# Cross attention ahead of a routed expert layer: the context used raw, its mean and deviation applied elsewhere

## The chip, the core and the metric

One core of a Trainium2 chip runs the whole program. The metric is device time in microseconds (us), the median of several executions. TensorE is written PE, VectorE DVE, ScalarE ACT, GpSimd POOL; SP (SyncE) issues most DMAs. All data is float32.

## The reference, cut to what matters

There are 32 batches of 100 query rows (256 wide) and 361 context rows (192 wide).

```
def layernorm(x, g, b):
    mu = jnp.mean(x, axis=-1, keepdims=True)
    var = jnp.mean(jnp.square(x - mu), axis=-1, keepdims=True)
    return (x - mu) * jax.lax.rsqrt(var + EPS) * g + b
x1 = layernorm(modality1, ln1_g, ln1_b)      # modality1 = layernorm of x
x2 = layernorm(modality2, ln2_g, ln2_b)      # modality2 = ctx_768, 32 x 361 x 192
q = x1 @ Wq + bq
k = x2 @ Wk + bk
v = x2 @ Wv + bv
scores = jnp.einsum('bqe,bke->bqk', q, k) * scaling
attn = jax.nn.softmax(scores, axis=-1)
ctx = jnp.einsum('bqk,bke->bqe', attn, v)
return ctx @ Wo + bo
```

The result is added to x. A second layer follows: a plain layernorm, one shared expert and 31 routed experts of which each row takes its best 3 (softmax over 31 logits, two 256 by 256 products with an exact gelu), summed and added.

## The kernel before, in words

The program has two stages. In the attention stage 37 numbered steps (-2 to 36, `STEPS`, line 275) are unrolled on each engine. Step i works on several things at once: the statistics of context batch i+2, the normalization of batch i+1, the scores of batch i-1, the softmax weights and the mix of batch i-2, and, for those steps in which a tile of 128 rows begins or ends (`starts`, `ends`, lines 106 and 110), the queries of a tile, the output of attention (`ends(i - 2)`), its layernorm (`ends(i - 3)`) and its routing (`ends(i - 4)`). Of the 32 batches 25 end a tile. After the stage come the 105 tiles of the routed experts and a final sum; the change leaves those alone.

Every engine works through its own instructions in order and waits on semaphores. What follows is the order within one step.

- SP (lines 341 to 371): loads context batch i+4 (288 KB, four buffers, line 322), the rows of a tile, in step 24 (`FILL_STEP`) a fill of 3.3 MB (line 349) with three small ones (lines 352, 353), in steps 1 to 23 one expert's first matrix and in steps 1 to 18 one expert's second matrix (256 KB each, lines 359, 365), and stores two tiles of 128 KB once DVE has made them (lines 370, 371).
- POOL (lines 505 to 536): the deviation of batch i+2 to the power -1/2 (lines 510, 512), the running mask sum (line 520), the same power for the output tile (lines 525, 527), and three indirect stores of 128 rows (line 535) for the tile of `ends(i - 4)`.
- DVE (lines 688 to 809): logits of a tile (701), statistics of context batch i+2 (705), layernorm of the output (724, which waits for line 527 of the step before), normalization of context batch i+1 into a buffer `z` (732, three instructions), normalization of x (743), aggregation of the statistics (763, 765), the routing mask (773), the row maximum of the scores (778), then, after the wait for the output product of PE, the output tile and the end of the routing (782 to 809).
- PE (lines 1015 to 1092): transposes of the softmax weights of batch i-2 (1026), six transposes of the normalized context of batch i (987, 988), scores (1039, 1040: 128 and 65 rows deep, the last row is a constant one that carries the key bias), the mix (1051, 1054), the query product, rank (1080, 1081, which wait for the mask of line 773), output product (1085, 1086) and logits.
- ACT (lines 573 to 635): copies PE's results to SBUF. Two copies of 361 columns carry the transposed context (595, 596).

Before step 0, DVE folds the biases into the key and value weights (`wk_aug`, `wv_aug`, lines 833 to 841) and PE multiplies query by key weights and value by output weights, so that a context row needs no product of its own.

## Time and profile before

| | us |
|---|---|
| median of 3 executions | 519.08 (519.04 to 521.75) |
| the profiled execution | 518.88 |
| its span in the trace | 517.1 |
| PE busy | 465.7 (90%) |
| DVE busy | 350.8 (68%) |
| POOL busy | 322.8 (62%) |
| ACT busy | 246.9 (48%) |

The span is what the trace shows between the first and the last instruction; the time of the same execution is 1.8 us longer. "Busy" counts instructions under way, and a busy PE isn't a PE at its peak. The shares are means over both stages. The page cuts the span into 40 slices of 12.9 us; the attention stage with its lead-in fills the first 18 or so.

### The profile page before, as it was taken

The numbers are of one execution on the slowest core, as the hardware profiler recorded it, in microseconds if no ns is written. First come the engines' busy times: TensorE is split into PE (matmuls) and PEld (weight loads), VectorE is DVE, ScalarE is ACT, GpSimd is POOL, SyncE is SP. The second block draws the span as 40 slices with busy tenths as digits, with TensorE's granted clock in tenths as the row PEclk, the third lists the DMA queues.
The fourth block names the chain that finished last, engine by engine and source line by source line (L and its number), as shares of the span: only waits on it lengthen the run. The fifth ranks groups of instructions, "written<-read, shape, count | busy, mean of one in ns | idle before, by whom it ended". The sixth has DMA issues, their size and how long they took to land.

```text
span 517.1 us, 13549 instructions
## 1 busy us (share of the span) xinstructions
PE 465.7 (90%) x3204; PEld 409.2 (79%) x3204; DVE 350.8 (68%) x1556; ACT 246.9 (48%) x821; POOL 322.8 (62%) x363
## 2 busy tenths in 40 slices
PE   1898889898888898888899999999999999999891
PEld 1787678687676777767798999989999999999891
DVE  4748788777868688657466766666666666661684
ACT  1355555646464565646344545545454545553220
POOL 6213756747567575657168888778888888885000
PEclk9989999989898999999999999999999999999997
DMA  7464766767565982569369999979888888875998
GB/s 240 125 194 125 250 207 194 237 187 231 191 200 181 324 291 94 168 208 320 97 122 189 187 186 189 185 132 145 136 138 138 135 138 137 138 116 83 332 349 305
DMA packets 80621, 97.53 MB, mean 189 GB/s; under 512 B 8689, under 2 KB 65298, under 8 KB 80546
## 3 DMA queue, kind: packets, MB, share of 16 engines
q1 hardware_dynamic: 60786, 70.79, 45.5%
q0 software_dynamic: 19472, 25.61, 29.3%
q8 instruction: 29, 0.48, 0.4%
q14 instruction: 46, 0.38, 0.3%
q10 hardware_dynamic: 288, 0.27, 0.2%
HBM read 54.91 MB, written 41.73 MB: 187 GB/s over the span
## 4 chain that ended last, share of the span: by engine, by line
PE 44%; DVE 7%; DMA 5%; SPq 4%; issue 3%; POOL 1%; ACT 1%; POOLq 0%; DVEq 0%
PE bank L1184 16%; PE bank L1195 15%; PE bank L1173 4%; DMA sum<-y_sb,token 3%; DMA w_all<-sum 2%; SPq L449 2%; SPq L450 1%; SPq L448 1%; POOL sum L557 1%; DVE w_all L732 1%; PE bank L1101 1%; DMA xt<-expert_rows_in 1%; PE bank L1085 1%; PE bank L1110 1%; PE bank L1051 1%
## 5 line engine op out<-in xcount | busy, mean ns | idle before, releaser
L557 POOL DMA_INDIRECT sum<-y_sb,token x105 | 169.8, 1617 | 48.6 <-issue 22.6
L643 ACT ACTIVATE up<-bank,b_all 128x128 f32<-128x128 f32 x260 | 81.4, 363 | 103.5 <-PE bank L1184 66.5
L1184 PE MATMUL bank<-xtt,w1b 128*128 128x128 f32 x840 | 111.2, 275 | 1.1 <-DVE w1b L913 0.8
L1195 PE MATMUL bank<-w_all,up 128*128 x420 | 108.6, 381 | 0.0
L1184 PEld LDWEIGHTS bank<-xtt,w1b 128*128 128x128 f32 x840 | 102.1, 192 | 1.7 <-ACT xtt L669 1.6
L921 DVE TENSOR_SCALAR y_sb<-bank,gate,inverse 128x256 f32<-128x256 f32 x105 | 57.1, 543 | 54.3 <-PE bank L1195 53.8
L535 POOL DMA_INDIRECT expert_rows_in<-xt,slot x75 | 74.6, 995 | 25.3 <-issue 25.0
L1195 PEld LDWEIGHTS bank<-w_all,up 128*128 128x128 f32 x420 | 71.7, 191 | 5.6
L913 DVE COPY w1b<-w_all 128x512 f32 x105 | 46.9, 447 | 18.2 <-PE bank L1184 8.0
L669 ACT ACTIVATE xtt<-bank 128x256 f32<-128x256 f32 x105 | 40.1, 383 | 38.3 <-PE bank L1173 37.7
L1173 PE MATMUL bank<-ident,xt 128*128 128x128 f32 x210 | 40.1, 273 | 0.2 <-DMA xt<-expert_rows_in 0.2
L1173 PEld LDWEIGHTS bank<-ident,xt 128*128 128x128 f32 x210 | 29.3, 141 | 11.4 <-DMA xt<-expert_rows_in 1.2
L512 POOL TENSOR_TENSOR rs<-rs,mhalf 128x4 f32<-128x4 f32 x32 | 33.2, 1036 | 2.5
L1051 PEld LDWEIGHTS bank<-w_all 128*128 128x128 f32 (+1 forms) x192 | 26.5, 192 | 9.3 <-ACT w_all L581 1.0
L600 ACT ACTIVATE tok<-bank 128x100 f32<-128x100 f32 x32 | 8.1, 253 | 53.5 <-PE bank L1054 53.5
L732 DVE TENSOR_SCALAR w_all<-w_all,mv,rs 128x192 f32<-128x192 f32 x96 | 32.3, 392 | 0.2 <-POOL rs L512 0.2
L608 ACT ACTIVATE w_all<-bank,negmax 100x361 f32<-100x361 f32 x32 | 17.9, 561 | 25.6 <-DVE negmax L778 25.6
L705 DVE BATCH_NORM_STATS2 c<-w_all 128x6 f32<-128x192 f32 x96 | 27.8, 345 | 3.4 <-POOL gates_all L494 3.4
L510 POOL TENSOR_TENSOR rs<-mv,eps_cols 128x4 f32<-128x4 f32 x32 | 6.7, 208 | 36.8 <-DVE mv L765 36.4
L1039 PE MATMUL bank<-w_all,tok 128*100 128x361 f32 x64 | 27.3, 512 | 0.0
L1110 PE MATMUL bank<-w_all,up 128*128 128x256 f32 x100 | 26.0, 382 | 1.5 <-DVE w_all L968 1.4
L1091 PEld LDWEIGHTS bank<-wr_s,tok 128*128 128x128 f32 x100 | 13.8, 193 | 17.0 <-ACT tok L616 16.6
(180 smaller groups left out, 938.3 us busy)
## 6 DMA issues: line engine op xcount, KB each, us to landing
xt<-expert_rows_in SPq DMA_DIRECT2D x105, 132.0 KB, 2.9
w_all<-in_w SPq DMA_DIRECT2D x47, 256.0 KB, 4.9
w_all<-in_ctx SPq DMA_DIRECT2D x32, 288.0 KB, 3.0
w_all<-sum SPq DMA_DIRECT2D x15, 384.0 KB, 7.4
sum<-pad_rows SPq DMA_DIRECT2D x1, 3328.0 KB, 12.0
w_all<-in_x SPq DMA_DIRECT2D x25, 128.0 KB, 3.3
sum<-y_sb SPq DMA_DIRECT2D x25, 128.0 KB, 3.7
sum<-xt SPq DMA_DIRECT2D x25, 128.0 KB, 3.8
```

The source lines that it names most:

```text
L512: pool.tensor_tensor(rs[s][:, 1, :], rs[s][:, 0, :], mhalf[:, :], ALU.pow).then_inc(ctx_rstd, 1)
L535: pool.indirect_dma_start(xs, bass.IndirectOffsetOnAxis(ap=slot[s4][:, k:k + 1], axis=0), h_sb[s4][:, :], None).then_inc(scattered[s4], 16)
L557: pool.indirect_dma_start(sums[s], bass.IndirectOffsetOnAxis(ap=token[sx][:, 0:1], axis=0), y_sb[sx][:, :], None, compute_op=ALU.add).then ...
L643: ins = act.activation(up[s][:, m * P:m * P + P], up_ps[s][:, m * P:m * P + P], ACT.Gelu, bias=b1_all[:, e, m:m + 1].rearrange("p o n -> p ...
L669: act.activation(xtt[s][:, :], tile_ps[s], ACT.Copy).then_inc(tile_t_copied, 1)
L732: ins = dve.tensor_scalar(z[s4][:, k, 0:D2], c_sb[s4][:, k, :], mv[s][:, k, 0:1], rs[s][:, 1, k:k + 1], ALU.subtract, ALU.mult)
L913: dve.tensor_copy(w1b[n.slot(2)][:, :], w1_all[:, bass.ds(e, 1), :].rearrange("p o n -> p (o n)"))\
L921: dve.tensor_scalar(y_sb[sx][:, :], down_ps[s], gate[s][:, 0:1], inverse[s][:, 0:1], ALU.mult, ALU.mult).then_inc(y_made, 1)
L1051: pe.matmul(mix_ps[:, 0:LQ], z[s4][0:KT[k], k, 0:P], probs_t[s][0:KT[k], k, :], start=(k == 0), stop=(k == 2))
L1173: mm = pe.transpose(tile_ps[s][:, c * P:c * P + P], xt[sx][:, c * P:c * P + P], ident[:, :])
L1184: mm = pe.matmul(up_ps[s][:, m * P:m * P + P], w[:, c * INTER + m * P:c * INTER + m * P + P], xtt[s][:, c * P:c * P + P], start=(c == 0), ...
L1195: mm = pe.matmul(down_ps[s], up[s][:, m * P:m * P + P], w, start=(m == 0), stop=(m == 1))
```

## The change

The context is no longer normalized row by row and no longer transposed on the core. The following comes in its place.

- The host also gives the context transposed (`ctxt`). SP loads it straight into the tiles that the scores read as keys (`load_ct`, 96 rows by two times 361), in three buffers, and the raw rows into six buffers (`load_ctx`, now batch i+3 in step i, once the mix of batch i-3 is made).
- The mean is taken out of the weights: `weights_with_bias` multiplies the key and the value weights by the layernorm's gain and subtracts each row's mean, so that a raw context row gives the same product as a centred one. It has four reductions over 192 columns and three small or medium instructions where there were two reductions. It runs for the keys before step -1 and for the values after step 0.
- POOL makes, beside the power -1/2, the deviation itself, twice (two more `tensor_tensor`): once as a row for the scores, once as column 192 of the raw context, where the constant one was.
- SP stores both rows (key deviation to the power -1/2, and deviation) to DRAM in runs of three numbers (`store_key_rows`), and loads them back in the next step: the first one to 100 partitions (`rb`), the second as the last row of the transposed keys (`load_key_rows`).
- DVE multiplies the scores by `rb` and takes the maximum in one instruction with SBUF output, then negates the maximum in a small one. ACT's exponential reads that output. ACT scales the transposed softmax weights by the power -1/2 (three instructions for two).
- Keys are dealt to the three blocks with a stride of 3 (121, 120 and 120 of them), and the width 192 is cut in 96 and 96 (+1) instead of 128 and 64 (+1).
- The 41 early expert loads are spread over 30 steps; one late load of four experts is merged into the one of step 33.

```
-        c_sb = [lend(2, P, 3 * D2).rearrange("p (t d) -> p t d", d=D2) for _ in range(SLOTS)]
-        zt0, zt1 = [lend(2, P, LK) for _ in range(2)], [lend(2, D2C, LK) for _ in range(2)]
-        z = [lend(2, P, 3 * (D2 + 1)).rearrange("p (t d) -> p t d", d=D2 + 1) for _ in range(SLOTS)]
+        ct = [lend(2, D2C, 2 * LK).rearrange("p (c j) -> p c j", c=2) for _ in range(CTS)]
+        c_sb = {s: lend(2, P, 3 * (D2 + 1)).rearrange("p (t d) -> p t d", d=D2 + 1) for s in (2, 3, 4, 5, 0, 1)}
...
             def load_ctx(b):
-                if b >= SLOTS:
-                    sp.wait_ge(ctx_norm, b + 1 - SLOTS)
+                if b >= CS:
+                    sp.wait_ge(mix_made, b + 1 - CS)
                     alone(sp)
...
+            def load_ct(b):
+                if b >= CTS:
+                    sp.wait_ge(scores_made, b + 1 - CTS)
+                    alone(sp)
+                sp.dma_start(ct[b % CTS][0:H, :, :], ctx_t[b].rearrange("(c p) j -> p c j", p=H)).then_inc(ct_in[b % CTS], 16)
+
+            def store_key_rows(b):
+                sp.wait_ge(ctx_std, 2 * b + 2)
+                alone(sp)
+                sp.dma_start(key_rows[b].rearrange("k (p t) -> p k t", t=3), rs[b % RS][:, 1:3, 0:3]).then_inc(key_rows_out, 16)
+
+            def load_key_rows(b):
+                sp.wait_ge(key_rows_out, 16 * (b + 1))
+                if b >= CTS:
+                    sp.wait_ge(max_made, b + 1 - CTS)
+                alone(sp)
+                sp.dma_start(rb[b % CTS][:, :], key_rows[b, 0, 0:LK].partition_broadcast(LQ)).then_inc(rb_in[b % CTS], 16)
+                sp.dma_start(ct[b % CTS][H:D2C, 1, :], key_rows[b, 1:2, 0:LK]).then_inc(ct_in[b % CTS], 16)
...
             def step(i):
-                if batch(i + 4) is not None:
-                    load_ctx(i + 4)
+                if batch(i + 3) is not None:
+                    load_ctx(i + 3)
                 if starts(i + 4) is not None:
                     load_x(starts(i + 4))
+                if batch(i + 1) is not None:
+                    load_ct(i + 1)
+                    load_key_rows(i + 1)
+                if batch(i + 2) is not None:
+                    store_key_rows(i + 2)
                 if i == FILL_STEP:
...
+                for w_all, w, e in EARLY[len(EARLY) * (i - 1) // EARLY_STEPS:len(EARLY) * i // EARLY_STEPS] if 1 <= i <= EARLY_STEPS else []:
+                    sp.dma_start(w_all[:, e, :], w[e]).then_inc(expert_in, 16)
...
@@ pool
+                    pool.wait_ge(ctx_rstd, b + 1)
+                    pool.tensor_tensor(rs[r][:, 2, 0:3], rs[r][:, 0, 0:3], rs[r][:, 1, 0:3], ALU.mult).then_inc(ctx_std, 1)
+                    pool.tensor_tensor(c_sb[b % CS][:, :, D2], rs[r][:, 0, 0:3], rs[r][:, 1, 0:3], ALU.mult).then_inc(ctx_std, 1)
...
@@ scalar
-                    act.activation(zt0[s], zt_ps0[:, 0:LK], ACT.Copy)
-                    act.activation(zt1[s], zt_ps1[0:D2C, 0:LK], ACT.Copy).then_inc(ctx_t_copied, 1)
...
+                    for k in range(3):
+                        ins = act.activation(probs_t[s][0:KEYS[k], k, :], probs_ps[0:KEYS[k], k * LQ:(k + 1) * LQ], ACT.Copy,
+                                             scale=rs[b % RS][0:KEYS[k], 1, k:k + 1])
...
@@ vector
-                    for k in range(3):
-                        ins = dve.tensor_scalar(z[s4][:, k, 0:D2], c_sb[s4][:, k, :], mv[s][:, k, 0:1],
-                                                rs[s][:, 1, k:k + 1], ALU.subtract, ALU.mult)
-                    ins.then_inc(ctx_norm, 1)
...
-                    dve.tensor_reduce(negmax[s][:, :], bank[s][0:LQ, 0:LK], AX.X, ALU.max, negate=True).then_inc(rowmax_made, 1)
+                    dve.wait_ge(rb_in[rated % CTS], (rated // CTS + 1) * 16)
+                    if rated >= 2:
+                        dve.wait_ge(probs_transposed, rated - 1)
+                    dve.tensor_tensor_reduce(probs[s][:, 0:LK], bank[s][0:LQ, 0:LK], rb[rated % CTS][:, :], 1.0, LOWEST, ALU.mult, ALU.max,
+                                             rowmax[s][:, 0:1]).then_inc(max_made, 1)
...
+                    dve.tensor_scalar(negmax[s][:, :], rowmax[s][:, :], -1.0, None, ALU.mult).then_inc(rowmax_made, 1)
...
+            def weights_with_bias(w_aug, bias, k):
+
+                for c in range(2):
+                    dve.tensor_tensor_reduce(bank[2 * k][:, c * D2:c * D2 + D2], w_aug[:, c, 0:D2], b2_row, 1.0, bias[:, c:c + 1], ALU.mult,
+                                             ALU.add, w_aug[:, c, D2:D2 + 1])
+                for c in range(2):
+                    ins = dve.tensor_tensor_reduce(bank[3][:, c * D2:c * D2 + D2], w_aug[:, c, 0:D2], g2_row, 1.0, 0.0, ALU.mult, ALU.add,
+                                                   wsum[k][:, c:c + 1])
+                then(ins)
+                then(dve.tensor_scalar(wmean[k][:, :], wsum[k][:, :], -1.0 / D2, None, ALU.mult))
+                for c in range(2):
+                    ins = dve.tensor_scalar(w_aug[:, c, 0:D2], bank[3][:, c * D2:c * D2 + D2], wmean[k][:, c:c + 1], None, ALU.add)
+                return ins
...
@@ tensor
-            def turn_ctx(b):
-                s4 = b % SLOTS
-                pe.wait_ge(ctx_norm, b + 1)
...
-                    pe.wait_ge(ctx_t_copied, b + 1)
+                    pe.wait_ge(ct_in[b % CTS], (b // CTS + 1) * 32)
...
-                    pe.matmul(bank[s][0:LQ, 0:LK], tok[:, 0, of_batch(b)], zt0[s], start=True, stop=False)
+                    pe.matmul(bank[s][0:LQ, 0:LK], tok[0:H, 0, of_batch(b)], ct[b % CTS][0:H, 0, :], start=True, stop=False)
```

## Rows read from the trace of the kernel before

**Rows 1.** The page's 40 slices of the span, and the first DMA queue.

```profile
PEclk9989999989898999999999999999999999999997
...
DMA  7464766767565982569369999979888888875998
...
GB/s 240 125 194 125 250 207 194 237 187 231 191 200 181 324 291 94 168 208 320 97 122 189 187 186 189 185 132 145 136 138 138 135 138 137 138 116 83 332 349 305
...
q1 hardware_dynamic: 60786, 70.79, 45.5%
```

**Rows 2.** Busy time by stretch: all scores, and five steps at the full clock.

```profile
core 0: us, PE busy (x) PEld busy (x) DVE busy (x) ACT busy (x) POOL busy (x), PEclk, DMA share, GB/s
...
20.95:223.46 202.51, 179.87 (x1264) 148.67 (x1262) 154.34 (x728) 110.55 (x411) 119.30 (x186) 0.96 0.64 203
...
186.99:218.80 31.81, 28.64 (x214) 23.60 (x212) 25.13 (x120) 18.40 (x71) 20.70 (x32) 1.00 0.46 154
```

**Rows 3.** Timeline of PE: start, duration, line; in brackets the wait.

```profile
20.95 0.77 PE L1039 MATMUL bank<-w_all,tok 128*100 128x361 f32 x2
...
131.42 0.27 PE L987 MATMUL bank<-ident,w_all 128*128 128x128 f32 x1
...
132.04 0.77 PE L1039 MATMUL bank<-w_all,tok 128*100 128x361 f32 x2
...
135.89 0.19 PE L1080 MATMUL bank<-mask,tri 128*128 128x31 bf16 x1 [1.08 <-DVE mask L773]
...
223.46 0.77 PE L1039 MATMUL bank<-w_all,tok 128*100 128x361 f32 x2
```

**Rows 4.** Timeline of DVE over two full steps.

```profile
133.37 0.95 DVE L732 TENSOR_SCALAR w_all<-w_all,mv,rs 128x192 f32<-128x192 f32 x3
...
135.40 0.28 DVE L765 BATCH_NORM_AGGREGATE mv<-c 128x2 f32<-128x6 f32 x3
...
135.59 0.24 DVE L773 TENSOR_REDUCE mask<-picks 128x31 bf16<-128x93 f32 x1
...
135.75 0.52 DVE L778 TENSOR_REDUCE negmax<-bank 100x1 f32<-100x361 f32 x1
...
137.11 0.17 DVE L782 RECIPROCAL rinv<-bank 128x1 f32<-128x1 f32 x1 [0.84 <-PE bank L1086]
...
142.33 0.25 DVE L773 TENSOR_REDUCE mask<-picks 128x31 bf16<-128x93 f32 x1
```

**Rows 5.** Timeline of POOL in the same stretch.

```profile
138.66 0.19 POOL L525 TENSOR_TENSOR rrs<-rmv,eps_cols 128x1 f32<-128x1 f32 x1 [1.41 <-DVE rmv L809]
...
139.67 1.04 POOL L535 DMA_INDIRECT expert_rows_in<-xt,slot  x1 [0.19 <-issue]
...
143.26 0.22 POOL L510 TENSOR_TENSOR rs<-mv,eps_cols 128x4 f32<-128x4 f32 x1
...
144.59 0.23 POOL L520 TENSOR_TENSOR msum<-msum,mask 128x31 bf16<-128x31 bf16 x1
```

**Rows 6.** DMA issues of the page: KB each, median us to landing.

```profile
w_all<-in_ctx SPq DMA_DIRECT2D x32, 288.0 KB, 3.0
...
sum<-pad_rows SPq DMA_DIRECT2D x1, 3328.0 KB, 12.0
```

**Rows 7.** Timeline of SP's DMA queue around the fill of step 24.

```profile
168.60 0.39 SPq L349 DMA_DIRECT2D sum<-pad_rows  x1
...
169.04 7.57 SPq L352 DMA_DIRECT2D sum<-pad_rows  x2
...
180.67 1.21 SPq L322 DMA_DIRECT2D w_all<-in_ctx  x1
```

**Rows 8.** Timeline of DVE during the folding of the weights.

```profile
9.40 0.42 DVE L834 CUSTOM_DVE_ANT_0 bank<-w_all,cols_s 128x192 f32<-128x192 f32 x1
...
9.74 0.49 DVE L837 CUSTOM_DVE_ANT_0 bank<-w_all,cols_s 128x256 f32<-128x256 f32 x1
```

More of the change, by code:

```diff
@@ L27 @@
 EPS = 1e-5
+LOWEST = -3.0e38
 SCALE = float(E) ** -0.5
-D2B = D2 - P
-D2C = D2B + 1
-KT = [P, P, LK - 2 * P]
+H = D2 // 2
+D2C = H + 1
+KEYS = [len(range(k, LK, 3)) for k in range(3)]
 TOKENS = B * LQ
@@ L194, in program @@
+        g1_s, bq_s, bk_s, bv_s = (cols_s[:, 2 * k:2 * k + 2] for k in range(4))
         uq = sb("uq", [P, 2])
         fold_q = sb("fold_q", [P, 2, D2 + 1])
-        fold_o0, fold_o1 = sb("fold_o0", [P, D1 + 1]), sb("fold_o1", [D2C, D1 + 1])
-        qs0, qs1 = sb("qs0", [P, 2]), sb("qs1", [D2C, 2])
+        fold_o0, fold_o1 = sb("fold_o0", [H, D1 + 1]), sb("fold_o1", [D2C, D1 + 1])
+        qs0, qs1 = sb("qs0", [H, 1]), sb("qs1", [D2C, 1])
+        wsum, wmean = two("wsum", [P, 2]), two("wmean", [P, 2])
@@ L239, in program @@
         x_in = sems(*[f"x_in{s}" for s in range(8)])
-        c_in = sems(*[f"c_in{s}" for s in range(SLOTS)])
+        c_in = sems(*[f"c_in{s}" for s in range(CS)])
+        ct_in = sems(*[f"ct_in{s}" for s in range(CTS)])
+        rb_in = sems(*[f"rb_in{s}" for s in range(CTS)])
         h_out = sems(*[f"h_out{s}" for s in range(SLOTS)])
@@ L271, in program @@
         sum_made, final_made, final_out = sems("sum_made", "final_made", "final_out")
-        MADE = 23
+        MADE = 19
         LATE = 21
         STEPS = range(-2, B + 5)
-        w1_order, w2_order = list(range(EARLY1)), list(range(EARLY2))
+        EARLY = [(w2_all, w2, e) for e in range(10)]
+        EARLY += [p for e in range(8) for p in ((w1_all, w1, e), (w2_all, w2, 10 + e))] + [(w1_all, w1, e) for e in range(8, EARLY1)]
+        EARLY_STEPS = 30
+        assert len(EARLY) == EARLY1 + EARLY2
         FILL_STEP = 24
-        EXPERT_DMAS = EARLY1 + EARLY2 + 8
+        EXPERT_DMAS = EARLY1 + EARLY2 + 7
         PADS_SP, PADS_POOL = range(0, 20), range(20, NE)
@@ L467, in _ @@
             const(pool.memset(eps_cols[:, 3:4], EPS * EPS / (1.0 + EPS)))
-            for s in range(SLOTS):
-                const(pool.memset(z[s][:, :, D2:D2 + 1], 1.0))
             const(pool.memset(ident[:, :], 0.0))
@@ L1029, in step @@
                     turn_x(starts(i))
-                if i > 0 and batch(i) is not None:
-                    turn_ctx(i)
                 b = batch(i - 1)
```

209 lines of the change are left out of this document (89 added, 120 removed).

## The prediction

> **What bounds the kernel now.** I read the page's 40 slices first: PE's granted clock, the share of the DMA engines and the bytes [rows 1]. The change touches only the attention stage. There the DMA engines work at 0.4 to 0.9 of their time, with one slice at 0.9 in the middle; nowhere for long at the limit. The table of stretches comes second: from the first scores to the last are 202.5 us, in which PE is busy 180, DVE 154, POOL 119, ACT 111 [rows 2]. No engine is full, so I look for a cycle. The timelines come third. Scores start at 20.95 for batch 0 and at 223.46 for batch 31 [rows 3]: 202.51 / 31 = 6.53 us per step.
>
> In a full step (all tile work present) the reader sees DVE without a gap except for one wait, at line 782, for PE's output product; and PE waits at line 1080 for DVE's mask [rows 3, 4]. From one mask to the next are 142.33 - 135.59 = 6.74 us: DVE's tail and head up to the mask, then PE's rank and output product, then DVE's tail again. That is the cycle. PE's own work isn't in it, except for the part from the mask to line 782. Once the clock was granted at 0.96 on average rather than 1.00 [rows 2]; over five undisturbed steps a step takes 31.81 / 5 = 6.36, so about 0.17 per step is the price of half-speed spells.
>
> POOL has a cycle of its own, close behind: from line 525 at 138.66 to the end of line 520 at 144.59 + 0.23 are 6.16 us of nearly gapless work, 3.6 of it for the three indirect stores (139.67 to 143.26) [rows 5]. Its statistics come from line 765, just before the mask [rows 4]. The cycle fits under 6.74 with 0.6 to spare. That slack is what the whole prediction turns on.
>
> **The change, part by part.** The sum is made against the profiled execution, 518.88 (span 517.1, 1.8 around it), 0.2 under the median.
>
> PE. Six transposes go: 132.04 - 131.42 = 0.62 us per step [rows 3], 19 us over 31. They stand where PE soon waits 1.08 for the mask, so on the path they are worth little in full steps. Narrower weight loads (97 and 97 for 128 and 65) are small: 0 to 0.15 per step, taken at 0. The strided reading of the softmax weights isn't in the trace: 0 to 0.3 per step (three transposes at the pace of the six are 0.3), taken at 0.
>
> ACT. Two copies go, three small instructions stand for two; ACT is busy 111 of 202 us [rows 2] and gets shorter. Nothing.
>
> DVE. Three normalizations go: 0.95 busy, about 0.9 in place [rows 4]. The row maximum, 0.52, becomes a reduction with a product. The nearest rows are line 834 with 0.42 for 192 columns and line 837 with 0.49 for 256 [rows 8]; by their slope 361 columns take about 0.60. It stands between mask and line 782, beside PE's rank and product (135.75 + 0.52 to 137.11, 0.84 of waiting [rows 4]), so it costs nothing until it grows by 0.8. The small negation, about 0.15, is in the cycle. The full cycle becomes 6.74 - 0.9 + 0.15 = 6.0. If only this counted, steps would be 0.75 shorter: 31 x 0.75 = 23 us.
>
> POOL. Two more products of three columns. Line 525, 0.19, is the nearest row [rows 5]; with the wait for the power before them I take 0.45 per step (0.2 to 0.7). POOL's full cycle becomes 6.16 + 0.45 = 6.6, over DVE's 6.0. DVE's line 724 waits for line 527 of the step before, so POOL now sets full steps, 25 of 32. In the others it has no stores and catches up: its mean is (25 x 6.6 + 7 x 1.8) / 32 = 5.6. Between 5.8 (POOL hidden by its catching up) and 6.6.
>
> SP. This is a new wait with a long queue behind it. Within step i-1, SP waits for POOL's deviation of batch i+1 (`store_key_rows`), and behind that wait stand the weights, the two stores, and the next `load_ctx(i + 3)`, which DVE needs at the start of step i+1. In the timeline POOL starts its power only after the stores, at 143.26, and ends at 144.6 [rows 5]; with the added products that is about 6.5 after the step's start (137.11 + 1.45). Then SP's issues: one store, one or two weights, two tiles, the load, some five at 0.4 (line 349 takes 0.39 [rows 7]), 2.2 in all, and 3.0 to land [rows 6], 4.5 under more load. Sum 11.7 to 13.2 for two steps, less 0.2: 5.8 to 6.5 per step where stores are on POOL in both. It lies on POOL's cycle, not beside it, so a late POOL delays the load too. Three buffers ahead of the mix don't help, since the queue is in order.
>
> DMA. Added per batch are 277 KB of transposed keys, 141 KB of `rb`, and 256 pieces of 12 bytes. 13.4 MB in all against 203 GB/s x 202.5 us = 41 MB now: by bytes, 0.64 of the engines' time becomes 0.64 x 54 / 41 = 0.85 [rows 2]. By packets, the first queue's take 0.455 x 16 x 517.1 / 60786 = 62 ns each [rows 1]; 292 long ones and 256 short ones of at most that are 1.1 to 2.1 us of 16 engines per step, 0.81 to 0.97. The early weights, spread out, take a little off. Hidden on average; transfers land later. The page "DMA: Bandwidth & Descriptors" of the Trainium skill says in "Why a DMA increments its semaphore by 16 and not by 1" that a transfer is split over the largest number up to 16 that divides its rows, so 100 partitions use 10 engines; and under "Specifications" that pieces under 512 bytes are read, modified and written. No trace of before shows either; both would put the first ten engines nearer to full, and by them I would set the step toward 6.6.
>
> I take 6.40 per step, the middle of 5.8 and 6.6 drawn up by the two chains meeting and by the half-speed spells, 0.17. Gain: 31 x (6.53 - 6.40) = 4. Bounds: 5.8 gives 23, 6.7 gives a loss of 5.
>
> The fill. Before, SP issues it at 168.60; the small one behind it is held for most of 7.57, and the next context load goes out only at 180.67, 12.1 later [rows 7]. That load is batch 29, read in step 27 (about 193): hidden. After the change the fill stands behind step 24's wait for POOL, so about 6.5 + 0.5 = 7.0 after DVE's start of step 24, and the load behind it is batch 28, which DVE reads in step 26, 2 x 6.4 + 0.2 = 13.0 after that start. It goes out at 7.0 + 12.1 + 0.8 (a weight) = 19.9 and lands at 22.9: a stall of 10 us of DVE, with PE idle soon after. Even counted from the fill's landing, 12.0 [rows 6], it is 19.0 + 3.0 - 13.0 = 9. If POOL has no stores ahead, 1.3 less; catching up gives back 1 to 2. Between 6 and 13; taken at 10.
>
> Start. The key weights take two more reductions (0.34 apart) and three instructions, some 1.7, before PE's first fold; the value folds leave PE's path, 2 us. Between -1 and 2, taken at 0.5. The late expert loads end before the experts start either way: 0, at most 2.
>
> Sum: 518.9 - 4 + 10 + 0.5 = 525.4; 525.5.
>
> **The rivals.**
>
> 1. DVE's cycle alone decides. POOL catches up in the seven short steps, SP's chain stays under two steps, and the step is 5.8. For it: POOL's mean of 5.6, and POOL idle 83 of 202 us now [rows 2]. Against: the short steps stand singly between runs of three or four full ones, where POOL loses 0.6 each. The fill then costs about 9, since DVE runs faster toward it. 518.9 - 23 + 9 = 505. Faster.
>
> 2. The fill is hidden as before, by a queue that holds more or by a DVE that is late itself, and the step is 6.4: 518.9 - 4 + 1 = 516. Against: the order of SP's issues is fixed, and rows 7 show it held.
>
> 3. The DMA engines become the bound (slower by more). One mechanism: `rb` and the keys land after PE's step i+2 wants them. It decides once landing takes longer than about 8 us. For it: slices at 0.9 even now [rows 1], and the fill at landing 12.0. Price: steps of 6.8, 31 x 0.27 = 8, and a fill of 12: 539.
>
> 4. The saving on PE counts fully, and more (PE no longer pushed to half speed): that is case 1 with 3 us more, 502. It goes with case 1. The opposite, more waiting on PE and so more half-speed spells (each costs about a microsecond where it meets a product), is within the 0.17 above.
>
> **How the numbers follow.** Forecast 0.48 (own range 519 to 533), rival 1 with 4 0.26, rival 2 0.12, rival 3 0.14. What the measurement can tell from no change is 0.5%, 516.5 to 521.7. Faster: 0.26 + 0.06 from rival 2 + 0.01 = 0.33. Same: 0.06 + 0.07 from the forecast's low end = 0.13. Slower: 0.40 + 0.14 = 0.54. The range reaches into rivals 1 and 3: 504 to 537.
>
> **What would show it.** Right: a wait of DVE's context statistics (or PE's idle time) of 6 to 13 us at step 26, a few us after the fill, released by a DMA of the context; POOL without idle time for DVE's aggregation in full steps; DVE waiting for POOL's power at line 724's successor; scores 6.3 to 6.5 apart elsewhere; the DMA share of the stage at 0.8 or more. Wrong: steps of 5.8 with DVE waiting only for PE (rival 1); no gap after the fill (rival 2); PE or DVE waiting for `ct` or `rb` in ordinary steps (rival 3). The forecast is wrong by more than its range if SP's chain misses two steps everywhere.

## The result, and the profile after

| | before | after |
|---|---|---|
| median, us (4 executions each, side by side) | 519.06 (513.79 to 521.75) | 561.21 (559.04 to 562.90) |
| ratio, 95% interval | | 1.086 [1.0798, 1.0922] |
| the profiled execution, us | 518.88 | 560.7 |
| its span | 517.1 | 558.1 |
| mean granted clock of PE | 0.977 | 0.935 |

Slower by 42 us. Ratios here and below leave disturbed runs out, so they aren't always the quotient of the medians. The forecast of 525.5 had the direction, and its range ended at 537.

The page after, read as [rows 1] were: PE's busy share by slice, PE's granted clock, the DMA engines, the first DMA queue.

```profile
PE   0898879688686872888889989999999999999992
...
PEclk9997897979989796699899999999999999999997
DMA  7888798879997899868944999998998888886998
...
q1 hardware_dynamic: 79714, 84.48, 56.9%
```

Two things catch the eye in slices 5 to 18: the DMA engines mostly at 0.8 to 0.9, where they were mostly at 0.5 to 0.7, and a clock below 0.9 in 7 of the 14. The first was expected, and it is the tempting culprit. The second goes with idle time of PE, which the next table shows: 183 us busy of 239.

The table of stretches, with the columns of [rows 2]: all scores (22.56 is the first, 262.04 the last), the part ahead of the fill, and the one step behind the fill.

```profile
22.56:262.04 239.48, 182.82 (x1091) 142.95 (x1091) 133.91 (x705) 91.12 (x350) 129.44 (x246) 0.87 0.86 225
22.56:205.06 182.50, 145.33 (x880) 113.76 (x880) 109.47 (x578) 73.54 (x282) 103.17 (x199) 0.90 0.88 219
205.06:226.67 21.61, 8.04 (x39) 6.41 (x38) 4.36 (x21) 2.86 (x11) 6.06 (x12) 0.67 0.99 306
```

The stage went from 202.51 to 239.48, or 37.0 of the profiled 41.8. The first scores start 1.6 later; what comes behind the last scores is 558.1 - 262.04 = 296.1 against 293.6, 2.4 more; the time around the span is 0.8 more. One step, behind the fill, takes 21.61. The other 30 take (239.48 - 21.61) / 30 = 7.26 each, against 6.53 before. So the ordinary steps are the larger part: 30 x (7.26 - 6.53) = 22, and the step behind the fill 15. DVE and ACT do 20 us less work each than before in the stage, POOL 10 more, and all of them wait more: no engine is busy all the time.

The list of waits after: engine, line, released by, total us, times, longest. PEld is PE loading the weights of a product.

```profile
ACT w_all L628 <- DVE negmax L801: 76.1, 31, 16.4
...
DVE rinv L797 <- PE bank L1108: 44.3, 21, 4.2
...
DVE c L725 <- DMA w_all<-in_ctx: 37.3, 14, 13.0
PEld bank L1113 <- ACT tok L636: 36.4, 24, 1.9
```

Three of them have a counterpart before, and all three have grown:

```profile
DVE rinv L782 <- PE bank L1086: 31.5, 22, 2.7
ACT w_all L608 <- DVE negmax L778: 25.6, 24, 3.0
...
PEld bank L1091 <- ACT tok L616: 16.6, 18, 1.7
```

They are ACT's wait for the negated maximum (L628, before L608), DVE's for PE's output product (L797, before L782) and PE's for ACT's copy of the transposed output tile (L1113, before L1091). New is DVE's wait for the context (L725). One part of it is on the page: a context load now lands 6.3 us after its issue (median) where it was 3.0 [rows 6].

```profile
w_all<-in_ctx SPq DMA_DIRECT2D x32, 289.5 KB, 6.3
```

The other part is in the waits of SP, which the page doesn't list (line 86 is a helper through which SP's waits pass):

```profile
SPq L86 <- DMA key_rows<-rs: 61.8, 26, 4.6
...
SPq L86 <- POOL w_all L540: 43.2, 19, 6.4
```

SP stands 61.8 us for the landing of the key rows that it has just stored, and 43.2 for POOL's second product of the deviation. Neither wait existed before, and everything that SP loads stands behind them.

Three timelines of one full step show how ACT's, DVE's and PE's waits hang together. DVE:

```profile
138.93 0.88 DVE L725 BATCH_NORM_STATS2 c<-w_all 128x6 f32<-128x192 f32 x3 [1.32 <-DMA w_all<-in_ctx]
...
141.00 0.50 DVE L792 CUSTOM_DVE_ANT_0 w_all<-bank,rb 100x361 f32<-100x361 f32 x1
141.43 0.08 DVE L792 DVE_READ_ACCUMULATOR2_ANT rowmax<- 100x1 f32 x1
142.56 0.17 DVE L797 RECIPROCAL rinv<-bank 128x1 f32<-128x1 f32 x1 [1.05 <-PE bank L1108]
142.65 0.13 DVE L801 TENSOR_SCALAR negmax<-rowmax 100x1 f32<-100x1 f32 x1
```

ACT, which waits for that negation:

```profile
142.81 0.60 ACT L628 ACTIVATE w_all<-w_all,negmax 100x361 f32<-100x361 f32 x1 [2.80 <-DVE negmax L801]
143.32 0.36 ACT L636 ACTIVATE tok<-bank 128x256 f32<-128x256 f32 x1
```

PE, which waits for ACT's copy:

```profile
141.93 0.60 PE L1108 MATMUL bank<-fold_o,tok 97*128 97x257 f32 x2
143.73 0.63 PE L1113 MATMUL bank<-wr_s,tok 128*128 128x31 f32 x4 [1.21 <-ACT tok L636]
```

The reader sees the maximum finished at 141.51 and its negation, 0.13 us of work, at 142.65. Between them DVE stands at L797, which waits for PE's output product. The negation has nothing to do with that product; it is only behind it in the code. ACT's exponential (L628) waits for the negation, ACT's copy of the transposed output tile (L636) stands behind the exponential, PE's logits (L1113) wait for the copy, and all of PE's next step stands behind the logits. Before, the maximum negated itself ahead of DVE's wait [rows 4]; ACT's exponential then started 0.8 us before DVE's reciprocal, which started at 137.11, and now starts 0.25 after it. The row of ACT before:

```profile
136.31 0.56 ACT L608 ACTIVATE w_all<-bank,negmax 100x361 f32<-100x361 f32 x1 [1.29 <-DVE negmax L778]
```

A new cycle has closed: PE's output product, DVE's negation, ACT's exponential and copy, PE's logits, PE's next step.

SP's queue and DVE around the fill, as in [rows 7]:

```profile
199.60 0.42 SPq L379 DMA_DIRECT2D sum<-pad_rows  x1
200.07 9.27 SPq L382 DMA_DIRECT2D sum<-pad_rows  x2
...
214.14 0.43 SPq L329 DMA_DIRECT2D w_all<-in_ctx  x1
```

```profile
218.43 0.88 DVE L725 BATCH_NORM_STATS2 c<-w_all 128x6 f32<-128x192 f32 x3 [12.98 <-DMA w_all<-in_ctx]
```

Here the forecast came true: the small fills are held for 9.27, the next context load goes out 14.5 after the fill (12.1 and one weight load were reckoned), and DVE stands for 12.98.

### The profile page after: what moved, and what is told of

Same layout as the page of the kernel before. It is cut to its first block, busy times and chain, and to the rows that moved or that the text cites. A ratio compares the mean times of both kernels' runs of the same rounds, so it can differ in the third digit from the quotient of the medians.

```text
span 558.1 us, 13352 instructions
## 1 busy us (share of the span) xinstructions
PE 467.8 (84%) x3012; PEld 401.3 (72%) x3012; DVE 331.7 (59%) x1535; ACT 226.7 (41%) x757; POOL 328.7 (59%) x423
## 4 chain that ended last, share of the span: by engine, by line
PE 44%; SPq 5%; DVE 3%; DMA 3%; issue 2%; ACT 2%; POOL 0%; POOLq 0%; DVEq 0%
PE bank L1203 16%; PE bank L1214 15%; PE bank L1192 4%; DMA w_all<-sum 1%; SPq L474 1%; SPq L472 1%; SPq L473 1%; PE bank L1107 1%; DMA xt<-expert_rows_in 1%; PE bank L1123 1%; PE bank L1076 1%; PE bank L1073 1%; PE bank L1059 1%; PE bank L1132 1%; PE bank L1058 1%
## 5 line engine op out<-in xcount | busy, mean ns | idle before, releaser
L585 POOL DMA_INDIRECT sum<-y_sb,token x105 | 165.5, 1577 | 53.8 <-issue 22.7
L945 DVE COPY w1b<-w_all 128x512 f32 x105 | 48.6, 463 | 18.5 <-PE bank L1203 7.9
L725 DVE BATCH_NORM_STATS2 c<-w_all 128x6 f32<-128x192 f32 x96 | 28.0, 347 | 40.6 <-DMA w_all<-in_ctx 37.3
L628 ACT ACTIVATE w_all<-w_all,negmax 100x361 f32<-100x361 f32 x32 | 19.1, 596 | 76.8 <-DVE negmax L801 76.1
L535 POOL TENSOR_TENSOR rs<-mv,eps_cols 128x4 f32<-128x4 f32 x32 | 6.7, 208 | 61.2 <-DVE mv L776 60.8
L1113 PE MATMUL bank<-wr_s,tok 128*128 128x31 f32 x100 | 18.2, 308 | 28.5 <-ACT tok L636 28.5
L1113 PEld LDWEIGHTS bank<-wr_s,tok 128*128 128x128 f32 x100 | 15.6, 222 | 36.5 <-ACT tok L636 36.4
L622 ACT ACTIVATE tok<-bank 97x200 f32<-97x200 f32 x32 | 10.8, 337 | 61.9 <-PE bank L1076 60.5
L1073 PEld LDWEIGHTS bank<-w_all 120*97 120x97 f32 (+1 forms) x192 | 25.6, 192 | 13.0 <-issue 5.0
L610 ACT ACTIVATE w_all<-bank,rs 120x100 f32<-120x100 f32 (+1 forms) x96 | 25.9, 341 | 14.5 <-PE bank L1046 13.8
L797 DVE RECIPROCAL rinv<-bank 128x1 f32<-128x1 f32 x25 | 4.2, 168 | 44.3 <-PE bank L1108 44.3
```

The costliest lines, as they stand in the source:

```text
L585: pool.indirect_dma_start(sums[s], bass.IndirectOffsetOnAxis(ap=token[sx][:, 0:1], axis=0), y_sb[sx][:, :], None, compute_op=ALU.add).then ...
L945: dve.tensor_copy(w1b[n.slot(2)][:, :], w1_all[:, bass.ds(e, 1), :].rearrange("p o n -> p (o n)"))\
L1073: pe.matmul(mix_ps[0:D2C, 0:LQ], c[0:KEYS[k], k, 0:D2C], probs_t[s][0:KEYS[k], k, :], start=(k == 0), stop=(k == 2))
L1113: mm = pe.matmul(logit_ps, tok[:, c, cut(t)], wr_s[:, c, :], start=(c == 0), stop=(c == 1))
```

## The experiments

Eighteen kernels ran, each timed in three rounds beside the kernel before. That kernel's own median differed from session to session: 518 to 519 in some, 531 to 532 in others, once at either level on the same chip. The changed kernel's didn't: 561.21 beside 519.06, 562.14 beside 531.23, and 560.82 for the one with filler beside 518.21. So a ratio holds within its session (the rows with one value of before). Whether a variant moves between the two levels, as before does, or stays, as the changed kernel does, was not measured, since none was run beside both. Differences between variants are therefore firm only between runs with before at one level; where they aren't, both readings are given, by the medians and by the ratios. The same holds for a single trace: the two of the changed kernel have 239.5 and 235.3 us in the stage, and 296.1 and 300.3 behind it.

| label | this, us | before, same session | ratio, 95% |
|---|---|---|---|
| a0_after_again | 562.14 | 531.23 | 1.0582 [1.052, 1.0643] |
| e1_fill_split | 560.98 | 531.65 | 1.0602 [1.0505, 1.0698] |
| e2_negate_early | 553.31 | 531.65 | 1.0417 [1.0343, 1.0491] |
| e3_no_round_trip | 544.65 | 531.65 | 1.0288 [1.0205, 1.0371] |
| e5_seven | 558.19 | 531.65 | 1.0458 [1.0336, 1.058] |
| e4_little_traffic | 563.81 | 531.23 | 1.0489 [1.0404, 1.0573] |
| b2_more_traffic | 531.27 | 531.23 | 0.9915 [0.9838, 0.9991] |
| e6_all_three | 538.07 | 531.23 | 1.0138 [1.0096, 1.018] |
| b3_negate_late | 549.09 | 518.93 | 1.0549 [1.0456, 1.0642] |
| e7_three_no_trip | 514.77 | 518.93 | 0.9931 [0.9888, 0.9975] |
| e8_three_little | 516.07 | 518.93 | 0.995 [0.9898, 1.0001] |
| e9_rows_on_act | 530.83 | 518.93 | 1.0219 [1.0126, 1.0313] |
| d1_negate_still_late | 549.25 | 531.59 | 1.0334 [1.0239, 1.0428] |
| d2_rows_first | 576.34 | 531.59 | 1.0829 [1.0731, 1.0927] |
| d3_no_trip_busy | 520.68 | 531.59 | 0.9818 [0.9732, 0.9904] |
| f1_three_busy | 536.71 | 518.21 | 1.0365 [1.028, 1.0451] |
| f2_after_busy | 560.82 | 518.21 | 1.0829 [1.0713, 1.0945] |
| f3_before_busy | 520.16 | 518.21 | 1.0041 [0.9997, 1.0085] |

### One part of the change undone at a time

**The fill in pieces.** The 3.3 MB fill goes as single tiles of 128 rows, one per step from step 4 on.

```
-                    sp.dma_start(sums[2].rearrange("(k p) n -> p k n", p=P), pad_rows...)
...
+                if 4 <= i < 4 + TILES + 1:
...
+                    sp.dma_start(sums[2][(i - 4) * P:(i - 3) * P, :], pad_rows[:, 0:D1])
```

> The changed kernel, with the 3.3 MB fill of step 24 cut into 26 pieces of 128 KB, one in each of steps 4 to 29. Theory Q (a context load is late whenever something long stands ahead of it in SP's queue): the 13 us wait of DVE at step 26 goes, and with it the half-speed spell behind it, 15 to 20 us in all; 543. Theory T (the DMA engines are simply too full): the bytes are the same, so little is gained, under 5 us; 557 or more.

560.98, where 543 was expected if the long wait mattered: nothing against 561.2 and 562.1. The wait of 13 us is gone (the longest of DVE for the context is 4.0), and the time isn't. The stage took 235.5, as in the second trace of the changed kernel (235.3), at a granted clock of 0.84 instead of 0.88, and other waits are longer: DVE's for PE's output product is 51.4, not 44.3.

**The negation ahead of DVE's wait**, right behind the maximum.

```
-                if rated is not None:          # behind the reciprocal, L797
-                    dve.tensor_scalar(negmax[s][:, :], rowmax[s][:, :], -1.0, None, ALU.mult)
+                    # behind the reduction, L792
+                    dve.tensor_scalar(negmax[s][:, :], rowmax[s][:, :], -1.0, None, ALU.mult)
```

> The changed kernel, with the negation of the row maximum moved from behind DVE's wait for PE's output product to directly behind the maximum. Theory N (the exponential waits for PE's output product through this instruction, and PE's logits wait for ACT behind it, 28 us in all, and these idle times call for half speed): at least 10 us less, 550 or below. If the late context loads alone set the steps: within 4 us of 561.

553.31: 8 to 9 us, a little less than the 10 expected. The waits tell where the rest went.

```profile
ACT w_all L628 <- DVE negmax L795: 43.1, 15, 12.8
DVE c L725 <- DMA w_all<-in_ctx: 41.6, 19, 12.3
PEld bank L1111 <- ACT tok L636: 14.4, 13, 1.7
```

PE's wait for ACT's copy falls from 36.4 to 14.4, below the 16.6 of before; DVE's wait for the context rises from 37.3 to 41.6 and comes 19 times, not 14. The next wait in line took over.

**No trip through DRAM.** Nothing is stored, and SP waits neither for POOL's deviation nor for a store's landing; in place of the two key rows, rows of the context are loaded, so the deviation is left out.

```
             def store_key_rows(b):
-                sp.wait_ge(ctx_std, 2 * b + 2)
-                sp.dma_start(key_rows[b]..., rs[b % RS][:, 1:3, 0:3])
+                pass
...
-                sp.wait_ge(key_rows_out, 16 * (b + 1))
...
-                sp.dma_start(rb[b % CTS][:, :], key_rows[b, 0, 0:LK].partition_broadcast(LQ))
+                sp.dma_start(rb[b % CTS][:, :], ctx_t[b, 0, :].partition_broadcast(LQ))
```

> The changed kernel without the key rows' trip: nothing is stored, and both loads of them read the host's transposed context in its place, at once (so the deviation is left out of scores and bias). The loads' bytes stay. Theory Q: SP never waits for POOL, context loads go out early, DVE's waits for them outside the fill go: 24 us and part of the half-speed spells, 530 to 540. Theory T: nearly as many bytes, so at most 8 us less.

544.65, 17 us, the largest single piece. DVE waits for the context 5.1 us in all instead of 37.3, at most 3.3 at once, so the fill delays it little. ACT still waits 53.2 for the negation.

**Seven context buffers**, loads one step earlier.

```
-            CS, CTS, RS = 6, 3, 6
+            CS, CTS, RS = 7, 3, 6
...
-                if batch(i + 3) is not None:
-                    load_ctx(i + 3)
+                if batch(i + 4) is not None:
+                    load_ctx(i + 4)
```

> The changed kernel with a seventh context buffer and each context load one step earlier (batch i+4 in step i, as before the change). Theory Q: DVE's waits for the context go, 24 us of them in ordinary steps and some 7 of the 13 at the fill: 530 to 540. Theory T: the wait moves to another load; 553 or more.

558.19: 3 to 4 us by the medians, 6 by the ratios (1.0458 against 1.0582, whose intervals overlap), where 530 to 540 was expected. DVE's wait for the context is down to 4.6, the fill's included, as without the trip; so by this comparison some 11 or more of e3's 17 us came from the trip in other ways than by this wait. SP still stands 66.0 us for the store's landing.

### Is it the DMA engines?

**The changed kernel with little traffic.** Keys and `rb` are loaded in full for the first three batches; later ones load one partition and use the older keys.

```
+                n = H if b < CTS else 1
+                sp.dma_start(ct[b % CTS][0:n, :, :], ctx_t[b]...[0:n])
+                n = LQ if b < CTS else 1
+                sp.dma_start(rb[b % CTS][0:n, :], key_rows[b, 0, 0:LK].partition_broadcast(n))
```

> The changed kernel with all its waits and the trip of the key rows, but from batch 3 on only one partition of the transposed keys and of the broadcast row is loaded (the others keep older values): 12 MB fewer. Theory T (full DMA engines make every transfer land late): transfers land in 3 us again, DVE's waits for the context go, 535 or less. Theory Q (the order of SP's issues behind POOL): the waits stay for the most part, 550 or more.

**The kernel before with dummy traffic**, 412 KB a batch into buffers that nobody reads.

```
+                    sp.dma_start(more_k[:, :, :], flat[0:96 * 2 * LK]...)
+                    sp.dma_start(more_r[:, :], flat[0:LK].partition_broadcast(LQ))
```

> The kernel before, with two loads per batch that nothing reads, of the size and row length of the transposed keys and the broadcast row (271 KB to 96 partitions, 141 KB to 100). Theory T: the stage's DMA share rises from 0.64 to 0.85, and the kernel loses most of what the change lost, 20 us or more. Theory Q: the transfers before are issued two steps ahead and stay hidden, within 6 us of before.

And the changed kernel as it is, beside both:

> The changed kernel itself, for comparison with kernels run beside it. The kernel before took 531.7 on the chip of the first experiments and 519.1 on the chip of the prediction. If that difference is one of the chip and falls on both alike, the ratio is 1.086 again.

563.81 with little traffic (its four executions scatter from 554.07 to 568.56), 562.14 as it is. 531.27 with the dummy traffic, 531.23 for the kernel before in that session. Rows of the stage, in the columns of [rows 2]. The changed kernel with little traffic, from its longest execution:

```profile
23.30:262.07 238.77, 180.97 (x1091) 141.16 (x1091) 133.87 (x705) 90.97 (x350) 130.08 (x246) 0.89 0.66 178
```

The kernel before with more traffic:

```profile
21.67:236.62 214.95, 188.53 (x1263) 155.27 (x1262) 155.09 (x728) 111.40 (x411) 119.51 (x186) 0.92 0.82 251
```

By the ratios little traffic is 1.0489 against 1.0582, with overlapping intervals: a DMA share of 0.66 instead of 0.86 gives back about 1%, and by the intervals anything from nothing to 2%, of a loss that is 6% beside the same runs of before. And 0.82 instead of 0.64 costs nothing against before in the same session. Full DMA engines alone aren't the cause, however plainly the page shows them. (The second row's stage, 215 us, is longer than in [rows 2]; that belongs to the sessions with before at 531, as far as can be told.)

### The negation alone, put into the kernel before

```
-                    dve.tensor_reduce(negmax[s][:, :], bank[s][0:LQ, 0:LK], AX.X, ALU.max, negate=True)
+                    dve.tensor_reduce(rowmax[s][:, :], bank[s][0:LQ, 0:LK], AX.X, ALU.max)
...
                     dve.reciprocal(rinv[m2][:, :], attn_ps[:, D1:D1 + 1])
+                    dve.tensor_scalar(negmax[s][:, :], rowmax[s][:, :], -1.0, None, ALU.mult)
```

> The kernel before with the change's placement of the negation alone: the maximum is taken without a sign, and a small instruction behind DVE's reciprocal (and so behind its wait for PE's output product) negates it. Theory N: the exponential and the logits behind it come later, and the kernel loses what e2 gave back, 5 to 15 us. If the placement only mattered in company of the other waits: within 3 us of before.

549.09 against 518.93: 30 us, 1.0549, for 32 instructions of 0.13 us, 4 us of work; 5 to 15 was expected. Nothing else was changed. Its waits:

```profile
ACT w_all L609 <- DVE negmax L787: 49.5, 28, 3.2
PEld bank L1096 <- ACT tok L617: 33.9, 24, 1.7
```

Both are the waits that grew in the changed kernel: ACT's doubled from 25.6, PE's from 16.6. This is the clearest single result: the place of the negation, by itself and with the DMA share at 0.58, costs 30 us where the whole change cost 42. By the traces 23 of these are in the stage (225.72 us against 202.51) and 8 behind the last scores (301.6 against 293.6), where the code is the same; the granted clock of the first 16.5 us there is 0.63, and was 1.00.

### The waits taken away together

**Split fill, early negation and seven buffers**, the three edits above.

> The changed kernel with the fill in 26 pieces, the negation directly behind the maximum and seven context buffers. If the three costs are separate: the sum of their single effects, 1.02 to 1.03 of before. If one common limit stands behind them (DMA engines, or half speed of PE): hardly below the best of the three alone, 1.04.

538.07, 24 us under the changed kernel in the same session, where the three singly gave 1, 9 and 4: waits stand in line and hide behind one another. What is late now:

```profile
PEld bank L1061 <- DMA w_all<-key_rows: 21.0, 14, 2.7
```

And what SP stands for:

```profile
SPq L86 <- DMA key_rows<-rs: 57.4, 25, 4.6
```

SP's wait for POOL is down to 6.4. What is left on SP is a loop of its own. In the timeline of its queue the loads of the rows go out 6.5 us (median) behind their store, and in 25 of 29 cases the next store follows within 0.8 us of them: store, landing, loads, next store. The stores are 7.07 us apart on average, and a step takes 216.06 / 31 = 6.97.

**The same without the early negation** (split fill and seven buffers).

> e6_all_three with the negation left where the change put it, behind DVE's wait for PE's output product (so the cut fill and seven buffers alone). e2 gave back only 0.016 with the other waits in place, b3 lost 0.055 alone. If the waits stand in line (each hides behind the longest): without the context waits the negation is worth more than in e2, and this is 1.03 or more against 1.014 of e6. If b3's loss belongs to the kernel before only: 1.02 or less.

549.25. In this company the negation is worth 10 to 11 us.

**e6 without the trip** (with the edit of e3; the deviation is left out).

> e6_all_three without the key rows' trip (both loads read the host's transposed context at once; the deviation is left out). In e6 PE waits 18 us for the key row and still is 1.014 of before. Theory K (the two transfers of the trip, one after the other, are what is left): 0.98 to 1.00 of before. Theory F (DMA engines, at 0.97 of the stage in e6, are what is left, since the loads' bytes stay): 1.01 or more.

**e6 with little traffic** (with the edit of e4).

> e6_all_three with one partition of the transposed keys and the broadcast row loaded from batch 3 on (12 MB fewer, older values kept), all waits and the trip as in e6. Theory F: the DMA share falls from 0.97 to about 0.75, transfers land sooner, 0.98 to 1.00 of before. Theory K: the waits for the key row stay, 1.01 or more.

514.77 and 516.07: 23 and 22 us under e6 by the medians, 10 to 11 by the ratios (0.9931 and 0.995 against 1.0138), since before was at 519 here and at 531 beside e6; the stage of the traces is 21 and 19 us shorter. The direction is clear, the size isn't. Taking away either the trip or the bytes is enough. In e6 the keys' last row arrives late, because it starts late (behind the landing of the store) and the store itself lands late while the DMA share of the stage is 0.97; with little traffic the loads of the rows go out 5.4 us behind the store instead of 6.5. Here, and in no other pair of runs, the traffic counts. The rows of the stage, e6 first:

```profile
22.70:238.76 216.06, 180.59 (x1090) 141.78 (x1089) 135.57 (x706) 92.16 (x353) 130.07 (x246) 0.89 0.97 245
```

And e7:

```profile
21.58:216.70 195.12, 170.74 (x1092) 135.12 (x1090) 135.73 (x708) 91.40 (x350) 129.39 (x247) 0.91 0.89 269
```

195.12 / 31 = 6.29 per step. POOL's timeline in e7 shows what sets some of the full steps:

```profile
119.94 0.21 POOL L536 TENSOR_TENSOR rs<-mv,eps_cols 128x4 f32<-128x4 f32 x1
...
125.47 0.96 POOL L564 DMA_INDIRECT expert_rows_in<-xt,slot  x1 [0.30 <-issue]
126.45 0.21 POOL L536 TENSOR_TENSOR rs<-mv,eps_cols 128x4 f32<-128x4 f32 x1
```

A full step of POOL that waits for no other engine is 126.45 - 119.94 = 6.51, and DVE waits for its power (`xt` for `rrs`) 13 times, 9.9 us in all. That is the POOL cycle which the forecast put at 6.6. In other steps POOL still waits for DVE.

### Three ways to win it back

**Key rows loaded by ACT's queue** (e6, the two loads issued by ACT after its step, the last key row first).

```
             def load_key_rows(b):
-                sp.wait_ge(key_rows_out, 16 * (b + 1))
+                act.wait_ge(key_out[b % CTS], 16 * (b // CTS + 1))
...
-                sp.dma_start(rb[b % CTS][:, :], ...)
+                act.dma_start(rb[b % CTS][:, :], ...)
```

> e6_all_three with the two loads of the key rows issued by ACT at the end of its step instead of by SP, through another queue, so that SP waits only for POOL and the row doesn't stand behind the bulk loads. Everything is computed. Theory K (time in the queue ahead of the rows): PE's 18 us of waiting go, 0.99 to 1.00 of before. Theory F: the row loads are no faster, 1.01 or more.

530.83, the lowest median of anything with the whole computation, and 6 to 7 us under e6 and its filled version (538.07, 536.71). By the ratio it is no better than e6 (1.0219 against 1.0138, before at 519 and at 531), and its stage in the trace is as long (215.92 against 216.06). So a gain isn't shown; it is still 2.2% over before in its session. PE's wait for the key row falls from 21.0 to 6.5, and in its place ACT stands 24.8 us for the store:

```profile
ACT w_all L607 <- DMA key_rows<-rs: 24.8, 8, 4.7
```

**Key rows first** (e6, SP loads them for the batch after next right behind the store, at the end of the step, and the keys after them).

```
-                    load_ct(i + 1)
-                    load_key_rows(i + 1)
...
+                if batch(i + 2) is not None:
+                    load_key_rows(i + 2)
+                    load_ct(i + 2)
```

> e6_all_three with another order on SP: in step i the store of batch i+2's key rows, weights and tiles, then at once the loads of the same rows and of its keys, one step earlier than in e6; the next context load follows. If lateness of the key rows is what is left: PE's waits for them (18 us in e6) go, 0.99 to 1.00 of before. If SP, which now waits for the store's landing once per step, becomes the bound: 1.01 or more, with waits for the context.

576.34, the slowest of all. The store goes out at 142.14 in one step; SP's queue issues nothing from 145.3 until the rows' load at 148.76, and every other load is behind it: DVE waits 42.1 for the context and PE 40.2 for the keys. SP's wait for the landing of the store, 57.4 us in e6, is 78.3 here. Moved ahead of the bulk loads, that wait costs more than late rows did.

**Filler on PE.** Six transposes per step that nobody reads, ahead of the scores: in e7 (deviation left out), in e6 and in the changed kernel; and three in the kernel before.

```
+                    for k in range(6):
+                        pe.transpose(bank[2 + k % 2][:, 0:P], ident[:, :], ident[:, :])
```

> e7_three_no_trip with six transposes of the identity per step put back on PE where the change removed six, with no reader and no wait (steps 4 to 31). If PE's work is off the cycle and its idle time calls for half speed: no slower than e7 (0.993), perhaps 1% faster, with a higher granted clock. If PE's work is on the cycle: 28 x 0.62 = 17 us slower at most, 1.01 to 1.03.

> The version with split fill, early negation and seven context buffers (1.0138 of before), plus six transposes of 128 rows that nobody reads, once per step ahead of PE's scores, as in the experiment without the trip. If idle time of PE is what brings the half-speed spells, and they hold back the rest, the slow spells (47.8 us in the stage there) shrink and the time falls by 0.01 to 0.015 of before: ratio 0.995 to 1.005. If PE's own time counts, 0.6 us more per step: ratio 1.03 to 1.05.

> The changed kernel as it is plus the same six transposes per step. If half-speed spells are a result of the waits that also lengthens them, the time falls by 1 to 2% against the changed kernel (its control: 562.1): 551 to 557. If the waits alone count, the same within 0.5%: 560 to 565. If PE is on the cycle, plus 31 x 0.6: 575 to 581.

> The kernel before plus three transposes per step that are overwritten by the real ones. In it PE is busy 180 of 202 us, with idle time only at the mask. If the transposes are absorbed by that idle time: within 0.5% or faster by up to 1% through a higher granted clock. If they stand on its path: 28 x 0.3 = 8 us, ratio 1.015.

The granted clock of the stage rises each time: 0.91 to 0.99 in e7, 0.89 to 0.93 in e6, 0.87 to 0.90 in the changed kernel. The time doesn't follow: 520.68 against 514.77 (6 us more), 536.71 against 538.07, 560.82 against 561.2 and 562.1, and 1.0041 [0.9997, 1.0085] in the kernel before. Only the last two comparisons have before at one level (519.06 and 518.21; 518.21). There the filler, 0.6 us of work per step and 17 us in all, or half of that, costs and earns nothing that can be told from noise. In the other two before was at different levels, and the readings differ: by the ratios the filler takes 6 us from e7 and adds 12 to e6, and the stage of their traces is 2.4 and 4.2 us longer. So filling PE isn't shown to be a remedy. What the clock would be worth without the filler's own work, and so whether the half-speed stretches are only a symptom of the waits, these runs don't tell apart.

## Why the prediction was right or wrong

- **PE: the six transposes "are worth little in full steps".** Right as far as shown. Put back into the changed kernel (f2) they cost nothing that can be measured, with a higher granted clock in the same sum.
- **DVE: three normalizations go, the reduction is about 0.60 and hidden.** Right: 0.50 and 0.08 for reading the accumulator, ahead of a wait of 1.05.
- **"The small negation, about 0.15, is in the cycle."** This step failed. The duration was right, 0.13. But it was priced by its own time on DVE. Its place wasn't read: it is behind the wait at L797, and ACT waits for it. The working named DVE and PE as the cycle and gave ACT one word, "Nothing", since it was busy 111 of 202 us. ACT's queue holds the exponential and, behind it, the copy that PE's logits need. Alone it costs 30 us (b3); inside the change, 8 to 11 (e2, and d1 against e6), since other waits lie beside it. Two lines of before pointed to it: ACT already waited 25.6 us for DVE's negated maximum, and PE 16.6 for ACT's copy.
- **POOL sets full steps at 6.6.** Only now and then in the changed kernel. Its line 535 starts at 135.70 and at 142.40, 6.70 apart and without a wait for another engine, but the next time only after 3.86 of waiting for DVE. In all POOL waits 60.8 us for DVE's aggregation, where it was 36.4, and DVE waits for POOL's power once, 0.3 us. In e7, with the other waits gone, POOL's full step is 6.51. The size was right and its turn seldom came. The step of 6.40 was likewise near what kernels without the other waits take (6.29 in e7, 197.39 / 31 = 6.37 in e8).
- **SP's chain, 5.8 to 6.5 per step, with `load_ctx` behind it.** This step failed too, and by size it is the larger miss inside the change. It was right in kind: SP waited for POOL (43.2 us), and DVE for the context in 13 ordinary steps, 24.3 us in all ahead of the fill. The landing was 6.3 where 4.5 was taken. But the chain had no term for SP's wait for the landing of the store, 61.8 us in 26 times, and the key rows' own way, from POOL through the store to `rb` and the last key row, was only in rival 3. The trip is worth 17 us alone (e3) and 10 to 23 in company (e7).
- **DMA share 0.81 to 0.97, "hidden on average; transfers land later".** Right: 0.86. The two rules that I weighed from the Trainium skill, page "DMA: Bandwidth & Descriptors" ("Why a DMA increments its semaphore by 16 and not by 1" and "Specifications"), would have set the step toward 6.6 through fuller engines. Little traffic in e4 gave back about 1%, so in the changed kernel neither was what counted most. Whether 100 partitions leave six engines free, and what pieces under 512 bytes do, no run here shows.
- **The fill, 6 to 13, taken at 10.** Right: 12.98, by exactly this chain. But taking the wait away gave 1 us (e1), and other waits took its place. A stall that is seen isn't always a gain that can be had.
- **Start +0.5**: 1.6. The expert stage 0, at most 2: 2.4, and 6.7 in the other trace of the same kernel.

In sum the terms came to 202.5 - 4 + 10 = 208.5 for the stage and it took 239.5. The fill's step, 21.6 against 6.4 + 10, is 5 of the 31 us that were missed; the ordinary step, 7.26 against 6.40 in 30 steps, is the other 26. So the miss is in the two steps named above, the place of the negation and the key rows' trip. That the fill's size came out inside its range is right by mechanism, but it didn't carry the result.

Of the rivals, 1 (DVE's cycle alone) and 2 (the fill hidden) fell at once with the first trace. Rival 3 had the direction, but neither what it should have been known by nor its mechanism: in the changed kernel PE and DVE have no listed wait for keys or `rb`, and DMA engines at 0.86 weren't the bound. Late key rows appear in e6 (21.0), mostly from what SP waits for ahead of its loads; bytes joined in visibly only there, once three other waits were away.

**What stays open.** Single gains of the undone parts are 1, 4, 9 and 17 us, 31 in sum. Together they gave 47 by the medians (from 562 to 515) and 34 by the ratios (1.0582 to 0.9931), so only for the first three (24 against 14) is more than the sum shown. Who hides behind whom was shown for the negation and the context load, not for every pair. Whether e9 gains at all stays open. A version with the whole computation and the deviation kept on the core (without a trip) wasn't built; e7, which leaves the deviation out, was 0.7% faster than before, with POOL setting some of its full steps.

## What to carry to other kernels

- Price a small instruction by what stands behind it, not by its duration. Ask of each new one: which wait is ahead of it on its engine, who waits for it, and what else is queued behind that one. Here 32 instructions of 0.13 us behind the wrong wait cost 30.
- A wait for a store's landing, at the head of the queue that also issues the bulk loads, belongs in the sum with its own term: here it held SP for 61.8 us.
- An engine that is half idle can still be in the cycle. Follow each result that changes hands through the idle engines as well, and read their waits before writing "nothing".
- When several waits are late by about the same, taking one away shows little. Take them away together, then put one back at a time; and before blaming a full DMA row, add the same traffic to the kernel that is fast.

## What the runs showed that was not expected

- PE's idle time shows in its granted clock. In the changed kernel's stage it was 0.87, so by an estimate from these means the lower of the two levels (1.2 and 2.4 GHz) held for 2 x 0.13 x 239.5 = 62 us, against 2 x 0.04 x 202.5 = 16 before. Behind the idle time of the fill the mean was 0.67 over a step.
- The kernel before has two levels of time, 518 to 519 and 531 to 532, steady within a session and not tied to the chip; the changed kernel doesn't (561.2, 562.1). The cause stays open.
- The landing of context loads doubled, from 3.0 to 6.3, at a DMA share of 0.86. The share alone doesn't explain it: with little traffic (e4) the share is 0.66 and the landing still 5.6. And dummy traffic that brought the kernel before to 0.82 had no measurable price. There the context is loaded two steps ahead of its use; that this is why it costs nothing is likely, but not shown.
